# Reordering TensorE's step of a fused attention and expert kernel: scores between the two halves of a tile's transposes

## What is computed

```python
x = x + attention(layernorm(x), ctx, ctx)       # softmax(q k^T / sqrt(8)) v per head, then Wo
# feed-forward:
logits = layernorm(x) @ Wr.T + br
expert = argmax(logits)
h = relu(layernorm(x) @ W1[expert].T + b1[expert])
out = x + h @ W2[expert].T + b2[expert]
```

## Time and profile before

| | us |
|---|---|
| median of 3 runs | 495.99 (495.71 to 498.73) |
| profiled execution | 498.64 |
| its span, first to last instruction | 496.8 |
| PE / PE weight loads / DVE / ACT / POOL busy | 460.0 / 348.5 / 408.5 / 312.9 / 240.6 |

### The profile page before, as it was taken

How to read it: one execution, slowest core, us unless ns; L and a number is a source line. 1 busy time by engine, 2 the same in 40 slices (tenths; PEclk the granted TensorE clock), 3 DMA queues, 4 the chain that set the end, 5 groups by cost and what they waited for, 6 DMA issues and landing times. The chain is left out here.

```text
span 496.8 us, 18730 instructions
## 1 busy us (share of the span) xinstructions
PE 460.0 (93%) x6467; PEld 348.5 (70%) x6467; DVE 408.5 (82%) x1061; ACT 312.9 (63%) x589; POOL 240.6 (48%) x390
## 2 busy tenths in 40 slices
PE   2999988899999999999999999989789999999990
PEld 1666644466666666666666666678779999999990
DVE  4999876677899998998989999956788878888870
ACT  1677776656666666666666666555557777777760
POOL 0548621222242554644645546355757654545451
PEclk9999999999999999999999999997999999999996
DMA  8356300001100111111111118432323332222100
GB/s 282 112 145 177 90 13 18 18 17 20 21 19 17 39 39 35 35 33 36 37 35 34 34 45 314 147 92 61 80 53 111 95 87 66 71 62 75 40 29 0
DMA packets 32752, 33.98 MB, mean 68 GB/s; under 512 B 6675, under 2 KB 26006, under 8 KB 32416
## 3 DMA queue, kind: packets, MB, share of 16 engines
q1 hardware_dynamic: 27840, 24.10, 18.6%
q0 software_dynamic: 4832, 8.80, 5.4%
HBM read 19.14 MB, written 9.99 MB: 59 GB/s over the span
## 5 line engine op out<-in xcount | busy, mean ns | idle before, releaser
L451 POOL TENSOR_TENSOR VP<-BIG,C 128x128 f32<-128x128 f32 x128 | 56.0, 457 | 131.1 <-PE PS L1020 125.1
L929 PEld LDWEIGHTS PS<-C,SB 128*128 128x128 f32 x512 | 53.7, 140 | 65.4 <-ACT SB L549 33.2
L701 DVE TENSOR_REDUCE MX<-PS 128x16 f32<-128x1024 f32 x64 | 78.2, 1222 | 23.4 <-PE PS L881 22.0
L473 POOL DMA_INDIRECT out<-SB,BIG x71 | 70.0, 986 | 52.7 <-DVE SB L854 44.4
L929 PE MATMUL PS<-C,SB 128*128 128x128 f32 x512 | 83.8, 286 | 6.3 <-ACT PT L532 5.3
L549 ACT ACTIVATE SB<-SB 128x1024 f32<-128x1024 f32 x64 | 67.6, 1057 | 20.5 <-DVE SB L709 18.9
L1041 PE MATMUL PS<-BIG,KM 128*128 128x128 f32 x568 | 78.6, 281 | 0.2
L709 DVE TENSOR_TENSOR SB<-PS,MX 128x1024 f32<-128x1024 f32 x64 | 77.4, 1209 | 1.7
L1054 PE MATMUL PS<-KM,SB 128*128 x568 | 75.7, 277 | 0.6 <-ACT SB L566 0.6
L466 POOL DMA_INDIRECT rows<-X,DESTI x64 | 64.3, 1004 | 19.6 <-issue 13.5
L1041 PEld LDWEIGHTS PS<-BIG,KM 128*128 128x128 f32 x568 | 71.4, 196 | 1.3 <-issue 1.1
(11 more groups left out here) (122 smaller groups left out, 699.7 us busy)
## 6 DMA issues: line engine op xcount, KB each, us to landing
BIG<-rows SPq DMA_DIRECT2D x71, 66.0 KB, 2.0
X<-in_x SPq DMA_DIRECT2D x16, 256.0 KB, 3.3
PT<-in_ctxT SPq DMA_DIRECT2D x16, 256.0 KB, 2.9
KM<-BIG SPq DMA_DIRECT2D x240, 16.0 KB
BIG<-in_we SPq DMA_DIRECT2D x1, 2576.0 KB, 10.4
KM<-in_w SPq DMA_DIRECT2D x1, 2048.0 KB
out<-SB,BIG POOLq DMA_INDIRECT x71, 2.3
rows<-X,DESTI POOLq DMA_INDIRECT x64, 2.5
```

Of the source, the lines that this page charges most:

```text
L451: last = nc.gpsimd.tensor_tensor(dst, v, own, ALU.mult)
L473: nc.gpsimd.indirect_dma_start(out=out, out_offset=bass.IndirectOffsetOnAxis(ap=RT[:, s.r, ID:ID + 1].bitcast(i32), axis=0), in_=YO[:, s.r ...
L701: nc.vector.tensor_reduce(MX[:, n % 2, :], sc, axis=AX.X, op=ALU.max).then_inc(mx_done, 1)
L929: last = nc.tensor.transpose(bank(4)[:, i * P:(i + 1) * P], SB[:, (n + 2) % 3, hp * P:(hp + 1) * P], ident)
```

## The change

In TensorE's step the row transposes move from the middle to the head. T0 of tile n-2 comes next, then the scores of tile n, then T1 directly behind the scores; the rest follows as before. The row transposes of a batch come one step later (`M_TR`), so they fall in even steps and the logits in odd ones. In ScalarE's step X1T's copy comes ahead of T0's copy, and the exponent is that of tile n-1 and stands between T0's copy and T1's copy. The square root of the last batches comes a step later. In VectorE's step the reciprocal goes ahead of the row maximum. `SOON` falls from 2 to 1, so that the routing of the last two batches and the second block table come a step later, and `STEPS` grows by one.

```diff
--- before.py
+++ after.py
@@ -86,7 +86,7 @@
 M_MOM = M_BN + ST - 1
 M_SEED = 18
 M_INV = (19, 20)
-M_TR = L_X1 + 2
+M_TR = L_X1 + 3
 M_LG = M_TR + 1
 M_TOP = 21
 M_HOT = 22
@@ -96,7 +96,7 @@
 INV_STEPS = 12
 RK = 2 * P + 2 * ST * E
 JS = 6
-SOON = 2
+SOON = 1
 STEPS = NT - ST + M_OUT - SOON + ST // 2
 LAST = NT - ST + M_POS - SOON
 F0 = NT + 3
@@ -527,9 +527,6 @@
                     act.wait_ge(od_done, n - 3)
                     need(act, ot_ready, n - 11)
                     nc.scalar.copy(NUM[:, (n - 4) % 8, :], bank(6)[:, P * (n % 2):P * (n % 2) + P]).then_inc(num_kept, 1)
-                if 2 <= n < NT + 2:
-                    act.wait_ge(pt_done, 2 * (n - 2) + 1)
-                    nc.scalar.copy(PT[:, n % 2, 0:4, :].rearrange("p a b -> p (a b)"), bank(4)).then_inc(pt_ready, 1)
                 for i in range(4):
                     j = s.batch(M_TR + 2 * i)
                     if j is not None:
@@ -537,16 +534,19 @@
                         need(act, lgp_done, 4 * j - 3 + i)
                         nc.scalar.copy(X1T[:, i].rearrange("p t d -> p (t d)"), bank(6)[:, 2 * P:4 * P]).then_inc(x1t_ready, 1)
                 if 2 <= n < NT + 2:
+                    act.wait_ge(pt_done, 2 * (n - 2) + 1)
+                    nc.scalar.copy(PT[:, n % 2, 0:4, :].rearrange("p a b -> p (a b)"), bank(4)).then_inc(pt_ready, 1)
+                if 1 <= n < NT + 1:
+                    act.wait_ge(sub_done, n)
+                    nc.scalar.activation(SB[:, (n + 1) % 3, :], SB[:, (n + 1) % 3, :], ACT.Exp, scale=SCALE).then_inc(exp_done, 1)
+                if 2 <= n < NT + 2:
                     act.wait_ge(pt_done, 2 * (n - 2) + 2)
                     nc.scalar.copy(PT[:, n % 2, 4:8, :].rearrange("p a b -> p (a b)"), bank(4)).then_inc(pt_ready, 1)
-                j = s.batch(M_SEED)
+                j = s.batch(M_SEED + 1)
                 if j is not None and j >= JS:
                     act.wait_ge(mv2, j + 1)
                     need(act, inv2_done, j - JS)
                     nc.scalar.activation(SD2[:], VAR2[:], ACT.Sqrt, bias=C[:, C_EPS:C_EPS + 1]).then_inc(sd2_done, 1)
-                if n < NT:
-                    act.wait_ge(sub_done, n + 1)
-                    nc.scalar.activation(SB[:, (n + 2) % 3, :], SB[:, (n + 2) % 3, :], ACT.Exp, scale=SCALE).then_inc(exp_done, 1)
             def ffn(part):
                 def stage(s):
                     whole = not isinstance(s.n, int)
@@ -696,13 +696,13 @@
                 n = s.n
                 stage3_early(s)
                 sc = bank(2 * (n % 2), 2).rearrange("p (h k) -> p h k", h=H)
-                if n < NT:
-                    dve.wait_ge(s_done, n + 1)
-                    nc.vector.tensor_reduce(MX[:, n % 2, :], sc, axis=AX.X, op=ALU.max).then_inc(mx_done, 1)
                 g, late = divmod(n - L_RD, GT)
                 if late == 0 and 0 <= g < NG:
                     dve.wait_ge(od_done, GT * g + GT)
                     nc.vector.reciprocal(RD[:, g % 2, :], bank(5)[:, P * (g % 2):P * (g % 2) + P]).then_inc(rd_done, 1)
+                if n < NT:
+                    dve.wait_ge(s_done, n + 1)
+                    nc.vector.tensor_reduce(MX[:, n % 2, :], sc, axis=AX.X, op=ALU.max).then_inc(mx_done, 1)
                 if n < NT:
                     dve.wait_ge(mx_done, n + 1)
                     need(dve, pt_done, 2 * (n - 2))
@@ -931,6 +931,22 @@
 
             def stage2(s):
                 n = s.n
+                turned = 0
+                for i in range(4):
+                    j = s.batch(M_TR + 2 * i)
+                    if j is not None:
+                        need(pe, num_kept, min(n - 3, NT))
+                        for t in range(2):
+                            last = nc.tensor.transpose(bank(6)[:, (2 + t) * P:(3 + t) * P], X[:, j * ST + 2 * i + t, 0:D], ident)
+                        last.then_inc(xt2_done, 1)
+                        turned = 4 * j + i + 1
+                m = n - 2
+                if 0 <= m < NT:
+                    pe.wait_ge(exp_done, m + 1)
+                    if m == 0:
+                        pe.wait_ge(xnt_ready, NG)
+                    need(pe, pt_ready, 2 * m)
+                    transposes(m, 0)
                 if 2 <= n < NT:
                     grp, t = divmod(n, GT)
                     if t == 0 and grp:
@@ -939,11 +955,8 @@
                     scores(n)
                 m = n - 2
                 if 0 <= m < NT:
-                    pe.wait_ge(exp_done, m + 1)
-                    if m == 0:
-                        pe.wait_ge(xnt_ready, NG)
-                    need(pe, pt_ready, 2 * m)
-                    transposes(m, 0)
+                    pe.wait_ge(pt_ready, 2 * m + 1)
+                    transposes(m, 1)
 
 
                 need(pe, x1_done, min(n - L_X1, NT))
@@ -981,19 +994,6 @@
                         last = nc.tensor.matmul(sums[:, (t + 1) * E:].rearrange("p (t e) -> p t e", e=E), COUNT[:, 1, :],
                                                 HOT[:, t:t + 1, :].to_broadcast([P, ST - t, E]), start=False, stop=t == ST - 1)
                     last.then_inc(rank_done, 1)
-                turned = 0
-                for i in range(4):
-                    j = s.batch(M_TR + 2 * i)
-                    if j is not None:
-                        need(pe, num_kept, min(n - 3, NT))
-                        for t in range(2):
-                            last = nc.tensor.transpose(bank(6)[:, (2 + t) * P:(3 + t) * P], X[:, j * ST + 2 * i + t, 0:D], ident)
-                        last.then_inc(xt2_done, 1)
-                        turned = 4 * j + i + 1
-                m = n - 2
-                if 0 <= m < NT:
-                    pe.wait_ge(pt_ready, 2 * m + 1)
-                    transposes(m, 1)
                 m = n - 3
                 if 0 <= m < NT:
                     if m == 0:
```

## The result

The changed kernel takes 502.95 us (502.46 to 503.15, 4 runs) against 495.85: a ratio of 1.0117, 95% interval 1.0073 to 1.0160. It is slower by 7.1 us, where I forecast +1.4. Its profiled execution took 503.12 us, with a span of 501.3.

The account below looks back on a forecast made before the run. PE's own list was taken to bound the middle, DVE close behind. Early steps -3.8, middle +4.0, reciprocal -0.3, tail +1.2, added step +0.3 gave +1.4: 497.4 us, own range 493.5 to 501, wide range 489.5 to 503.

Parts of the forecast that it names:

- rival 2: A late subtraction holds ScalarE's exponent, then T1's copy, in every fourth step; +6.5 us, 504; chance 0.12.
- T1 behind the scores: T1 comes 1.52 us after T0, over the 1.34 that T0, its copy and hand-overs take; the 0.18 stall goes.
- Row transposes at the head: Even steps from 12 to 66: row transposes wait for the NUM copy, a new unhidden stall of 0.45 us each.
- Sum of a middle pair: Middle stretch: odd plus even step 8.18 against 7.92 us, bounded 8.03 to 8.33, taken 8.15; +4.0 over 44 steps.
- Early steps: Before tile 12's scores: steps 4 to 7 take 3.12 us and gain 0.84 each; sum -3.9, taken -3.8 (to -2.0).
- Exponent a tile later: ScalarE: exponent runs one step after its scores, T1's copy follows to 2.9 us, needed at 3.9; costs nothing.
- Reciprocal ahead: VectorE: same work, frees the next group's denominators, one short wait in 8 steps; with Steps 56 to 63, -0.3 us.
- Steps 56 to 63: These steps hang on DVE, which also works on the block table; together with the reciprocal's move -0.3 us.
- Tail: Steps 64 and 65, without scores: T1 waits 1.34 us behind T0, +1.2 (0 to 2.2); the added step +0.3.
- The base: Profiled execution of 498.64 us, 2.65 above the median of 495.99; +1.4 gave 500.0, shifted to 497.4.
- The weight loads as a measure: Middle stretch: the skill's rule judges PE by weight loads (67% busy, DVE 93%), making DVE the engine to watch.
- Rival 1: Middle reaches DVE's floor of 3.83 us a step if the head's wait costs nothing; about 485, or 487.5; chance 0.10.

Follow-up runs that it names:

- second profile of the kernel before: The kernel before run once more with no edit; 496.66 us (10 runs), ratio 1.0016; its profiled execution took 495.99 us.
- Experiment 1: Changed kernel with the row transposes behind T0 and X1T's copy behind T0's copy on ScalarE; 492.27 us, ratio 0.9907 to the kernel before.
- experiment 6: Kernel before with only the exponent of tile n-1 moved between ScalarE's two copies; 495.81 us, ratio 0.9986.
- experiment 2: Changed kernel with the exponent of tile n back at the end of ScalarE's step; 556.8 us, ratio 1.121 to the kernel before.
- experiment 5: Kernel before with only the reciprocal moved ahead of the row maximum; 497.17 us, ratio 1.0014.
- experiment 3: Changed kernel with the reciprocal back behind the row maximum on VectorE; 512.16 us, ratio 1.0309 to the kernel before.
- experiment 9: Kernel before with the reciprocal ahead of the maximum and the exponent between the copies, TensorE's order untouched; 494.60 us, ratio 0.9954.
- experiment 7: Kernel of experiment 1 with T1 back behind logits and ranking in steps 64 and 65; 492.66 us, ratio 0.9911 to the kernel before.
- experiment 8: Kernel of experiment 1 with lines 961 and 965 moved between the V product and the denominators; 511.17 us, ratio 1.0281 to the kernel before.

## Why the prediction came out as it did

The sign was right and the size was a fifth: +1.4 against +7.1. The wide range (489.5 to 503) held the time by 0.05 us; the forecast's own range (493.5 to 501) did not. The wide range reached so far to make room for rival 2, which did not come about, so that it held the time is luck. Point by point, against the second profile of the kernel before:

- *T1 behind the scores.* Right. No T1 in the middle waits for its copy; the distance is 1.02 throughout.
- *Row transposes at the head.* Right in mechanism and size: 1.00 from the denominators, as worked out from the row of step 65, a stall of 0.45 against T0's 0.55. Experiment 1 took it away and gained 10.7 us.
- *Sum of a middle pair.* This is the term that was mis-sized. Taken 8.15, measured 8.34, just above the upper bound of 8.33; over 44 steps +8.0 and not +4.0. I called the new seams unknown, saw that seams differ by about 0.1, and then chose a value below the plain sum of 8.18. The new order has one change of shape more in each step (full transposes to 64-row scores), and it took 0.09. That nothing in the trace shows this seam was wrong: tile 3 of the kernel before has it (74.35 to 74.94). With 0.09 a step the plain sum is 8.36, the middle comes to +8.6, the early steps to some -3.1 and the whole to some +6.7, an estimate from these rows, close to the +7.1 measured.
- *Early steps.* -2.8 and not -3.8: the same seam makes such a step 3.21 and not 3.12, and the scores of tile 4 begin at 79.86, 0.31 later than worked out. The DMAs did not hold the scores of tile 8, which begin at 92.71, 3.21 after those of tile 7, like their neighbours.
- *Exponent a tile later.* Right that it cost nothing; experiment 6 finds nothing in the old order. But I priced it as a free extra, and in the new order 54 us hang on it (experiment 2).
- *Reciprocal ahead.* "The same work, one short wait in 8 steps" fell. In the old order it gains nothing alone (experiment 5), in the new one it is worth 9.2 us (experiment 3), and with the exponent between the copies about 2 us for both (experiment 9). What it is worth depends on when PE asks, and the change moved that by 0.54.
- *Steps 56 to 63.* +0.7, not -0.3: in the changed kernel they take 4.23 each, hardly more than the middle's 4.20, and VectorE waits for scores there too (2.2 us), so they hung on PE's steps and not on VectorE.
- *Tail.* +1.2, against +1.2 and +0.3. The reason given for it is not shown: experiment 7 removed T0's ring there and showed no gain in the medians. The rest, with the routing one step later, was not taken apart.
- *The base.* I compared with a profiled execution that held 2.6 us of lower clock and shifted to the median by that. This was sound, but the row of the table that showed it (0.94) I did not use.
- *The weight loads as a measure.* By weight loads PE is busy for 65% of the changed kernel's middle (120.2 of 184.6 us) and VectorE for 86%. Judged by weight loads, as the Trainium skill has it in "Perfetto Trace Analysis", section Identifying the Most-Contended Engine (the floating-point work done, which it names beside them, was not worked out), the engine to watch is again VectorE. The runs say PE's order, waits and seams, so here the rule leads astray; the matmul row (95% busy) shows 8.5 us of the gaps' 9.9. The bank rule of the Trainium skill, "PSUM — Partial Sum Buffer", was not tried against; experiment 1 keeps the wait and hides it.

Rival 1's floor of 3.83 a step was not reached by any order tried; the best middle, experiment 1's, takes 175.0 us for 44 steps, 3.98 each. Rival 2 did not come about: on the page of the changed kernel the 64 exponents wait 0.0 us in all. A chain like it is seen only with the exponent at the end of ScalarE's step (experiments 2 and 5).

## What to carry to other kernels

When a group is moved to the head of an in-order list, ask what its waits were covered by before; one group of 0.5 us put in front of it was worth 10.7 us here. Order by shape as well as by dependence: in a kernel of many small matmuls each change from full to 64-row or 32-column work is a term of the sum, and the trace of the kernel before may already hold its price. And price small moves together with the order they serve: two edits that alone gave nothing in the old order were worth 54 and 9 us in the new one, and the kernel with the lowest median took the new order only where the rows showed TensorE idle.

## What the runs showed of the hardware

Going from full matmuls to 64-row or 32-column ones took TensorE 0.08 to 0.11 us at the full clock in four places, and in the rows looked at the weight loads then begin with the matmuls and not ahead of them. A change to 32 columns and back, twice in each pair of steps, took 0.33 a step (experiment 8), and how the way back comes to more than the way there is open. And the granted clock fell to its lower level for 6.8 us in one profiled execution of a kernel and not in the other, after 7.0 us with almost the same activity (PE busy for 5.28 and 5.26); the two differ by 2.6 us.
